# Layer 3's attention: order of VectorE's work within a tick, and the distance from a tile's division to its output

## The reference

```python
def _L3_attn_ref(x, W_qkv, b_qkv, W_out, b_out):
    T, B, D = x.shape
    qkv = x @ W_qkv + b_qkv
    q, k, v = (to_heads(t) for t in jnp.split(qkv, 3, axis=-1))
    scores = jnp.einsum('bhqd,bhkd->bhqk', q, k) / jnp.sqrt(jnp.float32(Dh))
    scores = jnp.where(causal, scores, -jnp.inf)
    attn = jax.nn.softmax(scores, axis=-1)
    context = jnp.einsum('bhqk,bhkd->bhqd', attn, v)
    return context.transpose(2, 0, 1, 3).reshape(T, B, D) @ W_out + b_out
...
h = _layernorm(x, axis=-1) * (1 + ca) + sa
x = x + ga * _L3_attn_ref(h, L3_attn_W_qkv, L3_attn_b_qkv, L3_attn_W_out, L3_attn_b_out)
```

## Time and profile before

| | us |
|---|---|
| median of 3 runs | 3071.94 |
| their range | 3065.12 to 3072.29 |
| profiled execution, its own time | 3077.18 |
| profiled execution, its span | 3075.1 |
| TensorE busy, share of the span | 2800.2, 91% |
| VectorE busy, share of the span | 2169.0, 71% |
| mean granted TensorE clock (share of full) | 0.974 |
| first maximum of layer 3's attention | starts at 2794.1 |
| last maximum | starts at 2986.1 |

### The profile page before, as it was taken

How to read it: one execution, slowest core, us unless ns; L and a number is a source line. 1 busy time by engine, 2 the same in 40 slices (tenths; PEclk the granted TensorE clock), 3 DMA queues, 4 the chain that set the end, 5 groups by cost and what they waited for, 6 DMA issues and landing times.

```text
span 3075.1 us, 68905 instructions
## 1 busy us (share of the span) xinstructions
PE 2800.2 (91%) x25404; PEld 1875.6 (61%) x25404; DVE 2169.0 (71%) x5846; ACT 1696.2 (55%) x4083; POOL 1050.4 (34%) x1444
## 2 busy tenths in 40 slices
PE   6999999989999999999997899999899979998885
PEld 2666666656666666666665555577666645555663
DVE  6888888855666566666666788565777767786557
ACT  3877777773333377766775666543245533333553
POOL 6778777721000001111112454222333311014313
PEclk9999999999999999999998999999999989999997
DMA  3111111132000011111114444000244431335630
GB/s 103 29 29 24 26 25 29 29 84 84 15 1 1 20 28 31 29 29 29 30 29 110 136 131 132 1 15 1 73 141 116 125 93 29 71 84 161 185 112 28
DMA packets 189980, 188.13 MB, mean 61 GB/s; under 512 B 14304, under 2 KB 166048, under 8 KB 188752
## 3 DMA queue, kind: packets, MB, share of 16 engines
q1 hardware_dynamic: 189648, 183.73, 22.8%
HBM read 130.36 MB, written 53.31 MB: 60 GB/s over the span
## 4 chain that ended last, share of the span: by engine, by line
PE 62%; DVE 21%; issue 6%; ACT 5%; POOL 2%; DMA 2%; SPq 2%; DVEq 0%; ACTq 0%; POOLq 0%
PE pb L175 56%; ACT big L947 4%; PE pb L644 3%; DVE big L2168 2%; DVE big L817 2%; DVE big L246 2%; SPq L1849 1%; DVE big L800 1%; ACT big L172 1%; DVE big L2657 1%; DVE big L191 1%; DVE big L728 1%; PE pb L577 1%; DMA big<-parts 1%; PE pb L2139 1%
## 5 line engine op out<-in xcount | busy, mean ns | idle before, releaser
L175 PE MATMUL pb<-big 128*128 128x128 f32 (+12 forms) x20220 | 2523.6, 332 | 162.1 <-DVE big L2168 58.8
L175 PEld LDWEIGHTS pb<-big 128*128 128x128 f32 (+4 forms) x20220 | 1570.0, 146 | 917.5 <-issue 546.8
L172 ACT ACTIVATE big<-pb 128x512 f32<-128x512 f32 (+7 forms) x1444 | 826.3, 619 | 595.2 <-PE pb L175 350.1
L172 ACT ACTIVATE big<-pb,big 128x512 f32<-128x512 f32 (+2 forms) x520 | 312.1, 624 | 634.3 <-PE pb L175 518.1
L2168 DVE TENSOR_REDUCE big<-pb 128x4 f32<-128x1024 f32 (+1 forms) x256 | 278.2, 1087 | 113.5 <-PE pb L175 110.2
L186 POOL TENSOR_TENSOR big<-big 128x128 f32<-128x128 f32 x224 | 99.1, 458 | 691.7 <-DVE big L183 691.7
L947 ACT ACTIVATE big<-big 128x256 f32<-128x256 f32 x512 | 254.1, 499 | 69.1 <-DVE big L822 67.4
L947 ACT ACTIVATE big<-pb,big 128x128 f32<-128x128 f32 (+1 forms) x512 | 255.6, 513 | 64.3 <-DVE big L802 64.0
L1026 POOL TENSOR_TENSOR big<-big 128x512 f32<-128x512 f32 x128 | 159.8, 1274 | 246.5 <-DMA big<-recip 246.5
L817 DVE CUSTOM_DVE_ANT_0 big<-pb,big 128x256 f32<-128x256 f32 x512 | 186.7, 421 | 79.9 <-PE pb L175 79.7
L1523 DVE SCALAR_TENSOR_TENSOR big<-pb,big 128x128 f32<-128x128 f32 x512 | 144.1, 344 | 139.2 <-PE pb L175 138.4
(11 more groups left out here) (136 smaller groups left out, 2317.8 us busy)
## 6 DMA issues: line engine op xcount, KB each, us to landing
big<-parts SPq DMA_DIRECT2D x96, 512.0 KB, 4.2
parts<-big SPq DMA_DIRECT2D x384, 96.0 KB, 2.3
big<-recip SPq DMA_DIRECT2D x64, 512.0 KB, 6.1
big<-comb SPq DMA_DIRECT2D x32, 512.0 KB, 8.6
parts<-big SPq DMA_DIRECT2D x192, 64.0 KB, 2.1
big<-gates SPq DMA_DIRECT2D x8, 1024.0 KB, 6.1
big<-in_wf SPq DMA_DIRECT2D x1, 3072.0 KB, 14.7
big<-scratch SPq DMA_DIRECT2D x1, 3072.0 KB, 16.9
```

Of the source, the lines that this page charges most:

```text
L172: return e.activation(o, i, f, bias=bias, scale=scale)
L175: return e.matmul(o, l, r_, start=start, stop=stop, skip_group_check=True)
```

## The change

In the same tick, VectorE now takes posts, qk and v pieces and y of tick t - 1 first, then the maxima of unit t, then the norm pieces of tick t - 1. "a" follows "back" by one tick and "c" by two (before: three and four), and the loop has 73 ticks in place of 77. y goes into ticks 42, 46, 50 and 54. `steps` returns no projection for t = -1, since VectorE now asks for tick -1 too. No instruction is added or removed.

```diff
-            lag, last = 4, 64 + 13
+            lag, last = 4, 64 + 9
...
-                found = [(t // 4 + ahead, p) for at, p, ahead in ((0, "qk", 3), (1, "split", 3), (2, "v", 2))
+                found = [] if t < 0 else [(t // 4 + ahead, p) for at, p, ahead in ((0, "qk", 3), (1, "split", 3), (2, "v", 2))
...
-                return [(step, (t - late) // 2) for step, late in (("back", 7), ("a", 10), ("c", 11))
+                return [(step, (t - late) // 2) for step, late in (("back", 7), ("a", 8), ("c", 9))
...
-                return [(t - 46) // 3] if t >= 46 and (t - 46) % 3 == 0 and (t - 46) // 3 < 4 else []
+                return [(t - 42) // 4] if t >= 42 and (t - 42) % 4 == 0 and (t - 42) // 4 < 4 else []
...
                 for t in range(last):
+                    for step, it in posts(t - 1):
+                        vector_post(e, step, it)
+                    for g, p in steps(t - 1):
+                        if p in ("qk", "v"):
+                            vector_piece(e, g, p)
+                    for c in y_at(t - 1):
+                        vector_y(e, c)
                     if t < 64:
                         rowmax(e, t)
-                    if t:
-                        for step, it in posts(t - 1):
-                            vector_post(e, step, it)
-                        for g, p in steps(t - 1):
+                    for g, p in steps(t - 1):
+                        if p not in ("qk", "v"):
                             vector_piece(e, g, p)
-                        for c in y_at(t - 1):
-                            vector_y(e, c)
```

## The result

| | before | after |
|---|---|---|
| median of five runs, same chip | 3072.29 | 3052.12 |
| their range | 3065.12 to 3078.08 | 3049.37 to 3053.01 |
| profiled execution, its own time | 3077.18 | 3051.29 |
| its span | 3075.1 | 3049.2 |
| first maximum of layer 3's attention | 2794.14 | 2790.75 |

The ratio is 0.9932 with a 95% interval of 0.9915 to 0.9949: faster, by 20.2 us between the medians, where 20 were forecast.

The account below looks back on a forecast made before the run. TensorE was taken to wait for banks of a three-bank ring that VectorE empties only behind the row maximum. 22.5 us won, less 1 and 1.5 for late stacks, gave 20: 3071.94 to 3052 us, range 3045 to 3062.

Parts of the forecast that it names:

- ruler: Layer 3's attention timed by the starts of its row maxima, one per tick; four ticks, a group, took 12.34 us before.
- steps 2 and 3: Banks of v and qk freed before "c" asks: following odd ticks 2.03 us for 2.81; v tick 2.85, qk tick 3.73.
- The wait for ScalarE: qk tick: the maximum queues behind VectorE's qk piece, which waits for ScalarE's half; 0.46 us behind what TensorE allows.
- Both even ticks: Ticks with v and with qk in a steady group: 2.85 us (before 3.16) and 3.73 (before 3.56).
- The norm pieces: Layer norm work in two groups before tick 20: four transposes add 0.5 us, so 11.1 us a group for 13.0.
- 8 to 20: Ticks 8 to 20, 40.26 us: first group wins 0.8 us, the next two 3.8 together; 4.6 less.
- The two stack terms: Late stacks of Q and K: 1 us once for the weights in SyncE's queue, 1.5 us for longer landings.
- 20 to 40: Ticks 20 to 40, 61.68 us: five groups of 10.6 us, 8.7 us less.
- 40 to 63: Ticks 40 to 63, 66.76 us: three groups of 11.1 with y, then shorter ones, 58.25; 8.5 us less.
- Drain: End of the attention: the second-last tile's "c" no longer waits for the last division's bank; 0.7 us less, between nothing and 0.86.
- oscillation: Skill's rule that short TensorE idling between matmul groups can make the clock oscillate, so the change would win clock; counted as nothing.
- Rival B: SyncE's copies become the bound: up to 11.5 us a group, 11 us less won, 3061 us; chance 0.17.

Follow-up runs that it names:

- the lags alone: Changed kernel with VectorE's old order, keeping the new distances of "a" and "c", y ticks and 73 ticks: 3071.8 us in one execution against 3072.9.
- loads late: Changed kernel with the two loads for the next stage issued by SyncE behind the last stack: 3051.46 us against 3073.61, ratio 0.9929.
- qk on ScalarE: The kernel of loads late, with ScalarE emptying both halves of the qk bank: 3050.22 us against 3073.61, ratio 0.9921.
- qk behind: Changed kernel with VectorE's qk piece put back behind the maximum: 3059.84 us in one execution.
- backs on ScalarE: The kernel of loads late, with the copies back issued from ScalarE's queue seven ticks behind their qk: 3045.15 us against 3069.67, ratio 0.9926.

## Why the prediction was right, and where its terms were off

- **The total: in part luck.** The prediction's stretches sum to 21.8 us of ruler, 19.3 with the stacks taken off; 23.6 came. With the end of the stage (0.7 forecast, -0.45 in the profiled execution) it is 23.2 for the 20.0 forecast. The medians differ by 20.2; that they hit the forecast within 0.2 proves no term, and where the other 3 us are no run tells. The five times of the kernel before lie 13 us apart.
- **The mechanism, steps 2 and 3: shown.** The bank waits are gone, both odd ticks are at 1.95 and 2.02 (forecast 2.03), and the parts taken one at a time add up to the whole (1.24 + 0.86 = 2.10 of 2.09).
- **The wait for ScalarE: shown.** Forecast as 0.46 us in the qk tick, it is 0.44 when it is taken away (3.57 against 3.13). The tick itself was put at 3.73.
- **Both even ticks were put 0.16 too long** (3.73 for 3.57, 2.85 for 2.69). I read TensorE's wait for the division as its idle time, 0.17. What it cost is the distance from "a" to qk. In the kernel before, "a" stands here, 0.49 ahead of the qk of the earlier trace rows:

```profile
2896.00 0.33 PE L2638 MATMUL pb<-big 128*128 128x128 f32 x1
```

  In the changed kernel the distance is 0.16 (2883.02, 2883.18 above), 0.33 less, and 0.34 less for v (0.50 to 0.16). From qk to ScalarE's start it is another 0.10 less (1.07 for 1.17), from v to the next maximum as well (1.20 for 1.30). For qk I had taken off the 0.17 alone; for v I had added its matmuls to a drain's tick and taken off 0.06. A group is 10.23 where I took 10.6. That is near the low end that I had named for TensorE alone (10.2), but reached another way: with the wait for ScalarE gone as well, the group is 9.80.
- **The norm pieces** were priced by TensorE's transposes, 0.5, for 0.63 measured, and cost that in another way. VectorE in ticks 16 and 17:

```profile
2837.35 1.21 DVE L2658 TENSOR_REDUCE big<-pb 128x8 f32<-128x1024 f32 x1
2838.49 1.11 DVE L246 TENSOR_SCALAR big<-big 128x128 f32<-128x128 f32 x4
2839.51 0.48 DVE L2672 TENSOR_SCALAR big<-pb,big 128x256 f32<-128x256 f32 x1
2839.90 1.21 DVE L2658 TENSOR_REDUCE big<-pb 128x8 f32<-128x1024 f32 x1
```

  The statistics make the tick behind the v tick 1.11 longer (3.13 for 2.02). TensorE does not wait for them, so the maximum that opens the qk tick is the late one: qk starts 0.41 behind it (2837.35, 2837.76) and not 1.51, "normed" (1.11) fills the time until ScalarE is done (2839.30) and 0.3 more, and the qk tick is 1.02 shorter (2.55 for 3.57). The transposes make the next one 0.53 longer (2.48 for 1.95). **8 to 20** gave 6.8 for 4.6, 2.2 more. Two groups won 0.37 more each. 0.84 lies in where I cut: the first set's 1.11 falls ahead of tick 12, into a group in which I counted no such piece. And that group won another 0.6 more than I gave it, 1.4 for 0.8.
- **The copies: right in kind, short in size.** The weight load was to cost 1 us once; it cost 3.9, since I counted the wait and not the clock behind it (1.55), and SyncE's twelve copies took 9.38 behind the load where the earlier trace rows has 8.34. That row was one of the shorter groups: from tick 20 to 40 the kernel before issued its twelve in 8.3 to 9.1 us, and once needed 11.5 with the two back (2875.93 to 2887.45), so the 10.2 of the prediction was no upper bound. For longer landings I took 1.5; they had a median of 4.6 for 4.3, the same longest of 5.9, and cost 0.4, in tick 39. The two stack terms together were 2.5, and 4.3 came.
- So **20 to 40** gave 6.3, which is the forecast's 8.7 less 2.5, by errors that cancel: 10.5 from the five groups, less 4.3. **40 to 63** gave 10.3 for 8.5: 0.4 again in each of the first four groups, and 0.1 in each of the last two. y cost 0.48 a group (10.71 against 10.23), forecast 0.5. Drain: at full clock 16.9 to 17.0 for 17.61, about 0.65 less, forecast 0.7 (the lags alone, 16.9; loads late, 2954.6 to 2971.6). The profiled changed kernel, at 0.91, doesn't show it; four more kernels have this 0.91 in the drain, one of them without any late stack, and its cause is open.
- **The rules of the Trainium skill.** Landings at a DMA share of 0.73 did not grow by the 1.8 us that were estimated from the Trainium skill (DMA: Bandwidth & Descriptors, Latency and other measured facts); the longest was 5.9, as before. And the granted clock stayed at 1.00 over the three groups from 2871 to 2902, with TensorE still idle for 0.47 in an odd tick, so the oscillation of the Trainium skill (TensorE: Matmul & The Clock Gate, A second HAM failure mode) isn't seen here either. In this stage of the changed kernel the clock fell behind the waits for stacks of 3.86 and 2.46 us, and in the drain.
- **Rival B** stood 0.4 us a group away. With qk on ScalarE, which would allow 9.80, and all copies in SyncE's queue it is the outcome.

**Open:** what made TensorE stand for 0.7 to 1.5 us in the middle of a unit's matmuls in the two kernels that issue copies back from ScalarE, and once (0.95) with qk behind. No wait is shown in front, and no run tells a cause.

## What to carry to other kernels

When an engine both empties banks that another engine waits for and does work that nobody waits for yet, put the emptying first; look then at what the emptying itself waits for (here ScalarE's half), and ask what else could fill that idle time. Add up the queue that feeds the loop before making the loop shorter: one that needs 10.2 of 12.3 us is free, and at 10.2 of 10.2 a load put into it was a stall, with a lower clock behind it. Take such a queue's need from all its groups and not from one. Read what a wait costs from the distance between the instructions around it, and not from the idle time alone. Measure a change of one stage from an event at its start to one at its end, and not by totals, whose part ahead of it differed by up to 9 us.

## What was not expected of the hardware

- SyncE's twelve copies out took 8.3 to 9.1 us in the kernel before (ticks 20 to 40, DMA share 0.63), 8.3 to 9.4 in the changed one (share 0.73), and 9.0 to 9.5 in four groups that follow each other without a pause (share 0.72). Issuing is a cost of microseconds in each group and differs between groups of the same copies; that it rises with the traffic is not shown.
- A stall of TensorE of 2.46 us cost 1.55 more in the tick behind it (granted clock 0.66 on average over 5 us), and one of 1.84 did the same (a tick of 5.11, backs on ScalarE). One of 1.82 with qk on ScalarE did not, and the tick behind it took its 2.26; nor did one of 2.71 with qk behind (granted clock 1.00, a tick of 3.13). So the length of the stall alone does not tell whether the clock falls.
- The same instructions ahead of the stage ended up to 9 us apart (2786.2 to 2795.4).
